# Half of the base matrix gathered and transposed in pairs 2 to 5, x loaded from ScalarE's queue, and no GpSimd drain at the end

## What is computed

```python
def _L0_cond_ref(x, adapter_ids, weight):
    w = weight[adapter_ids]
    return jnp.einsum('bsi,boi->bso', x, w)

def _L0_ffn_ref(x, W_base, b_base, W_router, lora_A, lora_B):
    ...
    logits = xf @ W_router.T
    probs = jax.nn.softmax(logits, axis=-1)
    topk_p, topk_i = jax.lax.top_k(probs, TOP_K)
    ...
    h = jnp.einsum('td,erd->ter', xf, lora_A)
    lora_out = jnp.einsum('ter,eor,te->to', h, lora_B, w) * SCALING
    base = x @ W_base.T + b_base
    return base + lora_out.reshape(x.shape[:-1] + (W_base.shape[0],))

x = x + _L0_ffn_ref(_L0_cond_ref(x, itok_B_0_15, L0_cond_weight), ...)
x = x + _L1_ffn_ref(_L1_cond_ref(x, itok_B_0_15, L1_cond_weights), L1_ffn_up, L1_ffn_down, L1_ffn_perm)
```

## Time and profile before

| | |
|---|---|
| median of 3 runs | 684.3 us |
| the profiled execution | 684.34 us |
| its span in the trace | 682.5 us |
| so outside the span | 1.84 us |
| TensorE busy | 641.7 us (94%) |
| VectorE, ScalarE, GpSimd busy | 277.4, 158.8, 128.2 us |
| start of the first adapter matmul | 19.80 us |
| end of the adapter matmuls | about 287 us |
| last matmul starts | 668.5 us |
| last DMA issue (store) | 671.98 us |

### The profile page before, as it was taken

One profiled execution on the slowest core, in us unless ns is written; L12 is line 12 of the kernel. 1 busy time (PEld: TensorE's weight loads), 2 busy tenths in 40 slices (PEclk: granted clock), 3 DMA queues, 4 the chain that ended last, 5 costly groups with the idle time before them and its releaser, 6 DMA issues.

```text
span 682.5 us, 10584 instructions
## 1 busy us (share of the span) xinstructions
PE 641.7 (94%) x3266; PEld 366.1 (54%) x3267; DVE 277.4 (41%) x714; ACT 158.8 (23%) x294; POOL 128.2 (19%) x194
## 2 busy tenths in 40 slices
PE   3899999999999999887999999999999999999992
PEld 3334434434333433374767676767676666666660
DVE  2046666666656666773212421214221225121220
ACT  3100000000000000344232633234333244323241
POOL 5000001111111100300222222222222222222201
PEclk9799999999999999979999999999999999999997
DMA  8998671459595959300222222222222222222200
GB/s 292 411 405 311 241 286 36 172 184 392 191 396 182 402 174 404 106 17 9 77 67 80 63 78 61 79 65 79 61 77 63 79 65 77 62 77 63 78 31 31
DMA packets 42298, 102.86 MB, mean 151 GB/s; under 512 B 8322, under 2 KB 17538, under 8 KB 42242
## 3 DMA queue, kind: packets, MB, share of 16 engines
q1 hardware_dynamic: 34370, 80.24, 32.8%
q0 software_dynamic: 6784, 21.51, 9.4%
q10 hardware_dynamic: 1088, 0.56, 0.3%
HBM read 93.89 MB, written 8.39 MB: 150 GB/s over the span
## 4 chain that ended last, share of the span: by engine, by line
PE 86%; DMA 5%; DVE 2%; issue 2%; SPq 1%; ACT 1%; POOL 0%; ACTq 0%; DVEq 0%; POOLq 0%
PE wide L423 27%; PE bank L505 18%; PE bank L555 9%; PE bank L510 8%; PE wide L546 7%; DMA ring<-adapters_dram 5%; PE bank L533 5%; PE bank L437 4%; PE bank L403 3%; DVE base_t L868 1%; PE bank L518 1%; PE bank L519 1%; PE bank L520 1%; SPq L227 1%; PE bank L443 1%
## 5 line engine op out<-in xcount | busy, mean ns | idle before, releaser
L423 PE MATMUL wide<-ring,x_in 128*64 128x512 f32 x1024 | 228.3, 599 | 7.9 <-DMA ring<-adapters_dram 7.6
L423 PEld LDWEIGHTS wide<-ring,x_in 128*64 128x64 f32 x1024 | 72.8, 137 | 148.0 <-issue 142.5
L505 PE MATMUL bank<-c_hi,base_t 128*128 128x512 f32 x496 | 142.8, 409 | 0.8 <-DVE base_t L868 0.8
L797 DVE STREAM_TRANSPOSE c_pair<-wide 32x256 f32<-32x256 f32 x240 | 107.1, 446 | 63.7 <-issue 34.3
L505 PEld LDWEIGHTS bank<-c_hi,base_t 128*128 128x128 f32 x496 | 86.3, 189 | 25.0 <-issue 11.7
L677 ACT ACTIVATE act_sb<-wide 128x512 f32<-128x512 f32 x128 | 66.3, 603 | 101.7 <-PE wide L546 101.7
L932 DVE TENSOR_TENSOR xres<-bank,xres 128x512 f32<-128x512 f32 x32 | 22.1, 691 | 162.7 <-PE bank L555 162.7
L510 PE MATMUL bank<-c_lo,base_t 128*128 (+1 forms) x248 | 77.0, 391 | 0.0
L376 POOL DMA_INDIRECT out_dram<-xres,row_out x32 | 34.4, 1075 | 208.3 <-DVE xres L932 208.3
L555 PE MATMUL bank<-act_sb,down_sb 128*64 128x512 f32 x256 | 62.0, 605 | 1.5 <-issue 1.5
L637 ACT ACTIVATE small<-small 128x1 f32<-128x1 f32 x16 | 3.2, 203 | 249.1 <-DVE small L833 249.1
(11 more groups left out here) (111 smaller groups left out, 477.0 us busy)
## 6 DMA issues: line engine op xcount, KB each, us to landing
ring<-adapters_dram SPq DMA_DIRECT2D x120, 512.0 KB, 7.1
x_in<-x_seq_dram SPq DMA_DIRECT2D x32, 256.0 KB, 7.6
up_raw<-up_dram SPq DMA_DIRECT2D x64, 64.0 KB, 2.3
down_sb<-down_dram SPq DMA_DIRECT2D x32, 128.0 KB, 2.3
ar_sb<-lora_a_router_dram ACTq DMA_DIRECT2D x1, 544.0 KB, 4.4
mix_sb<-mix_dram SPq DMA_DIRECT2D x32, 16.0 KB
xres<-xT_dram,row_in POOLq DMA_INDIRECT x32, 3.4
out_dram<-xres,row_out POOLq DMA_INDIRECT x32, 3.1
```

Source lines behind the costliest of these rows:

```text
L423: last = pe.matmul(acc[half][h][z * TOK:(z + 1) * TOK, :], x_in[:, half, z, k, :], ring[:, k, z, h * HALF:(h + 1) * HALF], start=(k == 0), ...
L505: pe.matmul(c_bank(g, j)[:, :], base_t[:, j, w, k, :], c_hi[:, k, :], start=(k == 0 and w == 0), stop=False)
L797: last = nc.vector.transpose(c_pair[r * SQ:(r + 1) * SQ, :, q * SQ:(q + 1) * SQ], wide[half][q * SQ:(q + 1) * SQ, :, :] .rearrange("p h (k ...
```

## The change

Three edits.

1. **Base matrix.** GpSimd gathers row groups 0 to 3 at the start, as before. Groups 4 to 7 are gathered one each after `keep_pair` of pairs 0 to 3. TensorE turns groups 0 to 3 ahead of pair 0, as before, and groups 4 to 7 in pairs 2 to 5, behind the router of the pair before. These pairs are therefore written out, and the loop covers pairs 6 to 13. ScalarE copies groups 4 to 7 back after the tanh of pairs 1 to 4. Groups 4 to 7 use one pair of PSUM banks (4 and 5) only.
2. **x.** ScalarE issues the x loads: those of pairs 0 and 1 as soon as the order is known, that of pair t+2 when all blocks of pair t are done, ahead of tanh(t). SyncE is left with the adapter blocks, and no longer waits for whole pairs.
3. **The end.** The block is opened with `no_gpsimd_drain=True`.

```diff
-        block = ctx.enter_context(nc.Block())
+        block = ctx.enter_context(nc.Block(no_gpsimd_drain=True))
...
-            def load_pair(t, half):
-
-                for z in range(2):
-                    seq = of_order(2, t, z, SEQS - 1)
-                    sp.dma_start(x_in[:, half, z, :, :],
-                                 x_seq[bass.ds(seq, 1), :, :, :].rearrange("a p k t -> p (a k) t")) \
-                        .then_inc(x_in_in[half], 16)
+            def load_pair(t):
+
...
-                for half in range(2):
-
-                    sp.wait_ge(block_done, (i * 2 + half - 1) * KT)
-                    load_pair(i * 2 + half, half)
+                load_pair(i * 2)
+                load_pair(i * 2 + 1)
...
+            for j in range(CS):
+                gather_base(j)
...
                 keep_pair(t)
+                if t < CS:
+                    gather_base(CS + t)
...
                 router(t - 1)
+                if turns is not None:
+                    turn_base(turns)
                 adapter_blocks(i, half, range(5, 8), landed)
...
-            for j in range(KT // 2):
+            for j in range(CS):
                 turn_base(j)
-            for k in range(KT // 2):
-                adapter_blocks(0, 0, [k], (16, 16))
-                turn_base(KT // 2 + k)
-            adapter_blocks(0, 0, range(KT // 2, KT), (16, 16))
+            adapter_blocks(0, 0, range(KT), (16, 16))
...
-            with pe.Fori(1, PAIRS // 2 - 1) as i:
+            for t in range(2, 2 + CS):
+                pair(t // 2, t % 2, CS + t - 2)
+            with pe.Fori(1 + CS // 2, PAIRS // 2 - 1) as i:
...
+            def next_x(t, half):
+                act.wait_ge(block_done, (t + 1) * KT)
+                load_x(t + 2, half)
...
-            with act.Fori(0, PAIRS - 1) as t:
+            act.wait_ge(order_ok, 1)
+            load_x(0, 0)
+            load_x(1, 1)
+            for j in range(CS):
+                keep_base(j)
+            for t in range(2 + CS):
+                next_x(t, t % 2)
                 tanh(t)
+                if 1 <= t <= CS:
+                    keep_base(CS + t - 1)
+            with act.Fori(1 + CS // 2, PAIRS // 2 - 1) as i:
+                for half in range(2):
+                    next_x(i * 2 + half, half)
+                    tanh(i * 2 + half)
+            tanh(PAIRS - 2)
```

More of the change, by code:

```diff
@@ L260, in load_pair @@
                         rows_of((1,))
-            load_pair(0, 0)
-            load_pair(1, 1)
+            load_pair(0)
+            load_pair(1)
             with sp.Fori(1, PAIRS // 2) as i:
-                for half in range(2):
-                    sp.wait_ge(block_done, (i * 2 + half - 1) * KT)
-                    load_pair(i * 2 + half, half)
+                load_pair(i * 2)
+                load_pair(i * 2 + 1)
             def load_up(j):
@@ L344, in _, with gather_base @@
             pool.wait_ge(perm_in, 16)
-            for j in range(KT):
+            def gather_base(j):
                 gather(base_rows[:, j, :, :].rearrange("p k o -> p (k o)"), w_base, perm_sb[:, j:j + 1], base_in[j])
+            for j in range(CS):
+                gather_base(j)
             def keep_pair(t):
@@ L447, in turn_base, with pair @@
                 pe.wait_ge(base_in[j], 16)
-                if j >= 2:
+                if j >= CS:
+                    pe.wait_ge(base_turned, j)
+                elif j >= 2:
                     pe.wait_ge(base_turned, j - 1)
-                transposes(base_ps[j % 2], [base_rows[:, j, k, :] for k in range(KT)], base_tr)
-            def pair(i, half):
+                transposes(base_ps[j % 2 if j < CS else 0], [base_rows[:, j, k, :] for k in range(KT)], base_tr)
+            def pair(i, half, turns=None):
                 t = i * 2 + half
@@ L464, in _ @@
             pe.wait_ge(ident_ok, 2)
-            for j in range(KT // 2):
+            for j in range(CS):
                 turn_base(j)
-            for k in range(KT // 2):
-                adapter_blocks(0, 0, [k], (16, 16))
-                turn_base(KT // 2 + k)
-            adapter_blocks(0, 0, range(KT // 2, KT), (16, 16))
+            adapter_blocks(0, 0, range(KT), (16, 16))
             pe.wait_ge(loads_ok, 1)
-            pe.wait_ge(base_turned, KT)
+            pe.wait_ge(base_turned, CS)
             pe.wait_ge(ar_in, 16)
@@ L641, in base_leading, with load_x, keep_base @@
                 nc.scalar.copy(base_t[:, j, 0, :, :], base_rows[:, j, :, :]).then_inc(base_hi_ok, 1)
-            for j in range(KT):
+            def load_x(t, half):
+                for z in range(2):
+                    seq = act.value_load(order[0:1, 2, bass.ds(t + z * PAIRS, 1)], min_val=0, max_val=SEQS - 1)
+                    act.dma_start(x_in[:, half, z, :, :],
+                                  x_seq[bass.ds(seq, 1), :, :, :].rearrange("a p k t -> p (a k) t")) \
+                        .then_inc(x_in_in[half], 16)
+            def next_x(t, half):
+                act.wait_ge(block_done, (t + 1) * KT)
+                load_x(t + 2, half)
+            def keep_base(j):
                 act.wait_ge(base_tr, j + 1)
@@ L646, in _ @@
                     last = nc.scalar.copy(base_rows[:, j, h * KT // 2:(h + 1) * KT // 2, :],
-                                          base_ps[j % 2][h][:, :].rearrange("p (k o) -> p k o", o=P))
+                                          base_ps[j % 2 if j < CS else 0][h][:, :]
+                                          .rearrange("p (k o) -> p k o", o=P))
                 last.then_inc(base_turned, 1)
-            with act.Fori(0, PAIRS - 1) as t:
-                tanh(t)
+            act.wait_ge(order_ok, 1)
[5 more added lines that the diff above has]
+                next_x(t, t % 2)
+                tanh(t)
+                if 1 <= t <= CS:
[5 more added lines that the diff above has]
+            tanh(PAIRS - 2)
             for j in range(0, 6):
```

## The result

The changed kernel takes 673.15 us (median of 4 runs, 671.79 to 674.32), the kernel before 684.46 us (4 runs). The ratio is 0.983, 95% interval 0.981 to 0.986: 11.3 us faster, where 12.7 were forecast (671.6 us). Two of its runs took 672 us at a mean granted clock of 0.994, two 674 us at 0.989; the profiled execution is of the second kind, 674.32 us with a span of 672.5.

A forecast was written before the change was run, and what follows sets the result against it. Bytes were taken to set the time until 42.71 us, TensorE (86% of the chain) after it. Start 6.2 + stalls 3.3 + drain 7.3 - transposes 4.1 = 12.7 us less, 671.6 us; forecast range 669.3 to 673.4, with clock and SyncE rivals to 677.5.

The forecast's parts named there:

- The drain: At the kernel's end: without GpSimd's drain, 7.3 us of the span go; bounds 0 and 7.3.
- The rival that it is only put off: At the end: the drain's work still delays completion outside the span, 7.3 us come back, 678.9 us; chance 0.12.
- The stalls of pairs 10 to 15: With x off SyncE's queue, ring loads come 2.5 to 3.8 us earlier; all three stalls go, 3.3 us won.
- The rival that it stays as late: SyncE's gap behind its loop's branch back grows, so the 3.3 us of stalls stay: 674.9 us; chance 0.07.
- The transposes: In pairs 2 to 5, four late groups on TensorE's path cost 1.02 us each, 4.1 us, without waiting for gathers.
- The slower rival: Late gathers land after 20 us or more, delaying pairs 2 to 5; at 21.5 us, 689.6 us; chance 0.03.
- The start: Four fewer early gathers (5.15), earlier ring load (0.3), no wait at pair 1 (0.7): pair 1 starts 6.2 us earlier.
- the prediction's own signs: Expected profile: for the start, pair 1's first adapter matmul at 36 to 37 us; wrong if it starts after 38.
- The first rival, the clock at the start: In pair 0, waits drop TensorE's clock: the start gains 2.7 us in place of 6.2, 675.1 us; chance 0.12.

The follow-up runs named there:

- e12_padded_loop: The changed kernel with 8 reads of order, never executed, put into a branch of SyncE's loop to lengthen its body; 673.12 us, ratio 0.981.
- e6_filler: The changed kernel with 40 transposes of the identity put into TensorE's 4.7 us wait for c_tok between the layers; 670.84 us, ratio 0.979.
- e10_two_fillers: The kernel of e9_x1_filler with 16 further identity transposes in the 2.06 us wait ahead of the first up matmuls; 669.57 us, ratio 0.977.
- e9_x1_filler: The changed kernel with x of pair 1 on SyncE's queue behind pair 0's blocks and 40 identity transposes in the c_tok wait; 670.50 us, ratio 0.978.
- e3_base_only: The kernel before with only the base matrix's half moved to pairs 2 to 5; x stays on SyncE's queue, drain stays; 683.98 us, ratio 0.998.
- e4_x1_on_sp: The changed kernel with x of pair 1 alone put back on SyncE's queue, behind pair 0's adapter blocks; 671.91 us, ratio 0.980.
- e2_x_only: The kernel before with only the x loads moved to ScalarE's queue; 681.76 us, ratio 0.994.
- e1_drain_only: The kernel before with only the GpSimd drain at the end left out; 678.61 us, ratio 0.989.
- e5_after_again: The changed kernel itself, run again on another chip beside other experiments; 672.96 us, ratio 0.982.
- e7_all_late: The changed kernel with all eight row groups gathered behind pairs 0 to 7, none at the start, x of pair 1 on SyncE's queue; 674.36 us, ratio 0.983.
- e11_six_late: The changed kernel with two row groups gathered at the start, six behind pairs 0 to 5, x of pair 1 on SyncE's queue; 671.96 us, ratio 0.980.

## Why the prediction was right

The measured 673.15 us lie in the stated range, 1.5 us above the forecast. Three of the four terms came out near their sizes; the start did not, and one term was missing.

**The drain** (7.3 us): right, 7.2 in the spans, 7.4 by the run with this edit alone (5.8 to 9.1 by its interval). The rival that it is only put off is refuted: the time stood 1.8 us above the span before and after.

**The stalls of pairs 10 to 15** (3.3): right, every pair from 6 on takes 16.00 us. The prediction had SyncE 2.5 to 3.8 us earlier; it was 8.5 us earlier (12.5 less 3.9), since the stop at the branch went as well, which the prediction had not foreseen: that SyncE ended up so far ahead was luck. The padded loop brings the stop back and leaves SyncE 5.4 us earlier, and no stall returns. That 2.5 to 3.8 us would have been enough follows from the largest stall, 1.50 us, but was not run. The rival that it stays as late fell.

**The transposes** (4.1): 3.5. The term was read off the distance of two starts, 1.02 us. In the changed kernel that distance is still 0.97 (64.86 to 65.83), but the pair's length grew by 0.87; a pair's length is the measure to use, and why the two differ is not shown. The error of 0.6 us hid a part of the next one. No wait for a gather: the four late ones were issued at 47.40 and 63.40 for pairs 0 and 1, within 0.3 us of the copies' end, and landed in 4.2 to 10.2 us for all eight, where 17 us were free. The slower rival had no ground.

**The start** (6.2): 4.5. This is the step that failed in its size. The sentence at fault is the one that x of pair 1, moved ahead of the adapter blocks, "changes the order alone", because its bytes went through before 42.71 anyway. They did, but what set pair 1's start in the changed kernel was no longer its own first load: it was pair 0's last block, and x of pair 1, which had stood behind that block in the queues, now stood ahead of it. By the prediction's own signs this step is wrong: it had pair 1 at 36 to 37 us, called itself wrong from 38 on, and the profile has 38.2. 0.52 MB are 1.3 us. With this, 5.15 + 0.3 + 0.7 - 1.3 = 4.85, against 4.5. The two kernels that differ in this alone have the block at 36.44 and 34.84, and over eight profiles the means differ by 1.4 us. Of the 0.3 us for SyncE's earlier first load hardly anything is seen: the load comes at 7.49 in place of 9.28, but the engines moved 220 GB/s in the first 10 us in place of 217, 0.1 us' worth. The rest is within what one kernel varies: the first router of the changed kernel starts at 46.91 and 46.57 in its two profiles, and at 46.81 and 46.29 in the padded and the first filler's kernel, which have the same start.

**The first rival, the clock at the start:** it did not happen. From its third block on pair 0 ran at full clock, 1.94 us a block, with a wait of about 0.6 us before each. The Trainium skill's rule that the prediction set beside this rival (TensorE: Matmul & The Clock Gate, section "HAM oscillation — how this bites in real kernels") is for a group shorter than the wait for its transfer. Here the group, 1.94 us, is three times as long as its wait, so the rule does not reach this case, and no run here tests it. Where the clock fell in the profiles of the two kernels, TensorE had stood idle just before: 4.97 and 4.88 us in the kernel before, 4.68 in the changed one. A wait of 2.06 us ahead of the first up matmuls was followed by a fall in the changed kernel (0.63 us each) and by none in the kernel before (0.39).

**What the sum left out:** the clock elsewhere. The prediction took everything behind the last pair as unchanged, a term put at nothing without a reason, and 1.7 us of the profiled difference were lost there. The stretch from the last router of the pairs to the last down matmul, against the mean granted clock in the 50 us that begin with it:

| kernel | clock | stretch, us |
|---|---|---|
| e10_two_fillers | 1.00 | 387.6 |
| e6_filler | 0.97 | 388.2 |
| e9_x1_filler | 0.97 | 388.4 |
| before | 0.93 | 389.4 |
| e3_base_only | 0.93 | 389.3 |
| e4_x1_on_sp | 0.93 | 388.8 |
| e12_padded_loop | 0.93 | 389.0 |
| e2_x_only | 0.90 | 390.0 |
| e1_drain_only | 0.86 | 391.2 |
| changed | 0.86 | 391.1 |
| e5_after_again | 0.86 | 390.9 |
| e7_all_late | 0.86 | 390.7 |
| e11_six_late | 0.86 | 391.4 |

The same instructions (but for the fillers) take up to 3.8 us more the longer the clock is down. The long fall is not of the change's making: e1_drain_only, which has the kernel before up to its end, has it too, and e12_padded_loop, which has the changed kernel's TensorE program, has the short one. The changed kernel's runs at 672 and 674 us, with mean clocks of 0.994 and 0.989, fit these two cases (672.18 us and 0.994 for e12_padded_loop, 673.78 us and 0.989 for e5_after_again), though only one at 674 was traced. That the first filler removes the first fall and the second the other is shown in the traced executions; one run of e6_filler, at 0.989, did not get the benefit. Why a given execution gets the short or the long fall is not shown, and stays open.

In all: 6.2 - 4.1 was forecast for the start and the transposes together, 2.1, and 4.5 - 3.5 = 1.0 came; the other 1.7 us by which the profiled spans fall short (10.0 for 12.7) are the clock. The medians fall short by 1.4 only, since two of the four runs had the better clock. The range (669.3 to 677.5) held. It was built for the clock in pair 0 and for a late SyncE; that it also covered the clock between the layers is luck.

## What to carry to other kernels

At a start that bytes bound, count the bytes ahead of the load that will gate after the change, not ahead of the one that gates now; and what can be loaded before the first data-dependent load can be asked for is free there, so it should stay. A wait between two stages costs more than itself if the clock falls behind it: filling a wait of 4.7 us with idle transposes gained about 2 us here, about as much as moving half a matrix did (1.6). Look at the branch back of a loop on the queue engine: here it stopped for 3.2 to 5.5 us when the body was long and for 0.2 when it was short, and code that never runs counted in its length.

## What the runs showed of the hardware that I had not expected

- **The branch back.** SyncE's loop stopped 3.8 to 5.5 us at its branch back in the kernel before, 0.2 us in the changed one, and 3.2 to 4.5 us with padding that is not executed; the instruction queue moved 44, 15 and 45 packets. The Trainium skill has this (Runtime: NRT & Kernel Launch, section "Instruction fetch mechanics": a taken branch to code outside what is held waits for a DMA of it), and the trace agrees, with those numbers.
- **A load of small rows under load.** The router's weights, 0.56 MB in rows of 544 bytes, landed after 17.4 us when issued amid the adapter loads, which took 8.0 us for 0.52 MB in rows of 4 KB on the other queue; in the kernel before, issued into nearly empty queues, it took 4.4 us. Whether the rows' size or the second queue made it slow was not separated.
- **GpSimd's drain.** 7.268 us in each of the three profiles that have it (before, e2_x_only, e3_base_only), with its last store landed before it, and nothing of it left when the instruction is not there.
